# Order of the o statistics, the gate and the split remainders in a gated linear attention and FFN kernel

## What is computed

```python
def step(state, inp):                      # over the 512 positions, per head
    state = state * exp(gt)[..., None] + vt[..., None] * kt[..., None, :]
    return state, einsum('bhvk,bhk->bhv', state, qt)
out = (out - mean) / sqrt(var + 1e-05) * gamma + beta     # over 128 channels
out = (out * silu(x @ Wg)) @ Wout
x = layernorm(x + out)
h = silu(x @ w1.T * s1) * (x @ w2.T * s2)
h = gelu(h @ h1.T * t1)
h = gelu(h @ h2.T * t2)
x = layernorm(x + h @ w3.T * s3)
```

## Time and profile before

| | |
|---|---|
| median of 3 runs | 178.25 us (177.07 to 178.44) |
| the profiled execution | 178.06 us, of it the span 176.3 us |
| granted TensorE clock, mean | 0.998 of full |
| TensorE busy | 160.1 us (91%), 778 matmuls |
| TensorE weight loads | 119.9 us (68%) |
| VectorE busy | 137.3 us (78%) |
| ScalarE busy | 116.8 us (66%) |
| GpSimd busy | 111.8 us (63%) |

### The profile page before, as it was taken

The page is one execution under the profiler, slowest core; times in us unless marked ns, Lnnn a source line. Parts: engine busy times, 40 slices in busy tenths (PEclk is TensorE's granted clock), DMA queues, the critical chain, the costliest instruction groups (busy, mean ns, idle before and its releaser), DMA issues.

```text
span 176.3 us, 2661 instructions
## 1 busy us (share of the span) xinstructions
PE 160.1 (91%) x778; PEld 119.9 (68%) x778; DVE 137.3 (78%) x278; ACT 116.8 (66%) x211; POOL 111.8 (63%) x109
## 2 busy tenths in 40 slices
PE   0899999999888999998999999899999999999980
PEld 0766667868656676876868678587666875887870
DVE  0689889967798997599999975999996695854062
ACT  5444789993236836187787468677978578995721
POOL 8707987969907779983477998919684250803132
PEclk9999999999999999999999999999999999999999
DMA  4999910244100000000000000000002000040102
GB/s 111 329 396 414 393 48 0 51 129 121 60 4 0 2 0 0 4 0 2 0 0 0 0 0 0 0 0 0 0 0 65 0 0 0 2 114 23 55 8 63
DMA packets 7455, 10.55 MB, mean 60 GB/s; under 512 B 753, under 2 KB 5394, under 8 KB 6930
## 3 DMA queue, kind: packets, MB, share of 16 engines
q1 hardware_dynamic: 6866, 7.50, 13.8%
q0 software_dynamic: 576, 2.88, 4.2%
HBM read 8.55 MB, written 1.84 MB: 59 GB/s over the span
## 4 chain that ended last, share of the span: by engine, by line
POOL 18%; PE 14%; DVE 13%; issue 12%; ACT 6%; DVEq 1%; POOLq 0%; ACTq 0%
POOL u_tok L345 7%; DVE state L1152 5%; POOL f_lo L406 4%; PE ffn L667 3%; POOL o_acc L360 3%; PE ffn L658 2%; DVE y L1164 2%; PE ffn L636 2%; PE ffn L641 1%; ACT last_f L1108 1%; PE att L580 1%; POOL o_rstd L368 1%; POOL r_rstd L368 1%; PE ffn L682 1%; ACT f_hi L938 1%
## 5 line engine op out<-in xcount | busy, mean ns | idle before, releaser
L1152 DVE TENSOR_TENSOR_SCAN state<-gate,att 128x512 f32<-128x512 f32 x32 | 38.4, 1209 | 0.8 <-PE att L580 0.8
L406 POOL TENSOR_TENSOR f_lo<-full,f_hi 128x512 fp32r<-128x512 f32 x18 | 23.0, 1293 | 20.2 <-DVE full L1238 14.9
L946 ACT ACTIVATE f_hi<-ffn,vec_cols 128x512 fp32r<-128x512 f32 x24 | 16.5, 686 | 19.8 <-PE ffn L667 19.6
L658 PE MATMUL ffn<-f_hi,h_hi 128*128 128x512 f32 x96 | 28.2, 407 | 0.2
L667 PE MATMUL ffn<-f_lo,h_hi 128*128 128x512 f32 x96 | 26.1, 398 | 0.0
L360 POOL TENSOR_TENSOR o_acc<-o_acc,y 128x512 f32<-128x512 f32 x16 | 20.6, 1290 | 8.6 <-DVE y L1164 8.5
L345 POOL TENSOR_TENSOR u_tok<-kv_tok 128x1024 f32<-128x1024 f32 x12 | 25.5, 2136 | 0.1
L580 PE MATMUL att<-ident,u_tok 128*128 128x128 f32 x128 | 20.2, 285 | 2.1 <-POOL u_tok L345 1.3
L658 PEld LDWEIGHTS ffn<-f_hi,h_hi 128*128 128x128 f32 x96 | 17.6, 188 | 5.8 <-ACT f_hi L946 1.5
L580 PEld LDWEIGHTS att<-ident,u_tok 128*128 128x128 f32 x128 | 15.7, 146 | 7.3 <-DVE state L1152 2.9
L667 PEld LDWEIGHTS ffn<-f_lo,h_hi 128*128 128x128 f32 x96 | 17.8, 188 | 3.7
(11 more groups left out here) (188 smaller groups left out, 354.5 us busy)
## 6 DMA issues: line engine op xcount, KB each, us to landing
h_raw<-in_hT SPq DMA_DIRECT2D x2, 1024.0 KB, 12.0
h_hi<-in_hT POOLq DMA_DIRECT2D x2, 1024.0 KB, 11.6
x_tok<-in_x SPq DMA_DIRECT2D x4, 256.0 KB, 4.7
out<-out_tok SPq DMA_DIRECT2D x3, 256.0 KB, 2.3
w_raw<-in_w12T SPq DMA_DIRECT2D x1, 512.0 KB, 4.3
w_hi<-in_w12T POOLq DMA_DIRECT2D x1, 512.0 KB, 8.6
q_swap<-q_hi SPq DMA_DIRECT2D x3, 128.0 KB, 2.5
q_swap<-q_lo SPq DMA_DIRECT2D x3, 128.0 KB, 2.4
```

Source lines behind the costliest of these rows:

```text
L406: nc.gpsimd.tensor_tensor(lo[:, o], full_block(layer, o), hi[:, o].bitcast(F32), ALU.subtract).then_inc(pool_rested, 1)
L658: nc.tensor.matmul(bank[:], h_hi[:, layer - 1, c, tile(o)], src_hi[:, c], start=(c == 0), stop=False)
L946: nc.scalar.activation(hidden[layer][0][:, o], bank[:], ACT.Gelu, scale=scales[:, 1 + layer, o:o + 1]).then_inc(gelu_hi_ready, 1)
L1152: nc.vector.tensor_tensor_scan(state[:, k % 3], gate[:, b], A[2 + k % 2][:], 0.0, ALU.mult, ALU.add).then_inc(scanned, 1)
```

## The change

`transpose_o` is put ahead of `center_o`, and the statistics and the aggregate of o ahead of `apply_gate`. Two remainders change engines: (1,1) goes from GpSimd to VectorE, behind `apply_gate`; (2,3) from VectorE to GpSimd, behind the last outer product of the next row. rest(2,1) goes behind `x2_normalise`. On TensorE, x2's transposes go ahead of the output's pass over the rounded parts, and the next row's second set of u transposes and its first replicated q go ahead of `ffn_out_rest`. Two waits on ScalarE guard the slot `full[:, 0]`, which (2,3) now shares with (1,0) and with the next row's first silu.

```diff
--- before.py
+++ after.py
@@ -236,8 +236,8 @@
         weight_groups.append((flat(w3_raw[:]), flat(w3_hi[:]), flat(w3_lo[:]), (w3_loaded, w3_hi_loaded)))
         WG = len(weight_groups)
         ALL_BLOCKS = [(layer, o) for layer in range(3) for o in range(OB)]
-        ON_POOL = [(0, 0), (0, 1), (0, 2), (1, 0), (1, 1)]
-        ON_DVE = [(0, 3), (1, 2), (1, 3), (2, 1), (2, 0), (2, 2), (2, 3)]
+        ON_POOL = [(0, 0), (0, 1), (0, 2), (1, 0), (2, 3)]
+        ON_DVE = [(0, 3), (1, 2), (1, 1), (1, 3), (2, 0), (2, 1), (2, 2)]
         hidden = ((f1_hi, f1_lo), (f2_hi, f2_lo), (f1_hi, f1_lo))
         LAYER_2_BANK = (0, 2, 3, 1)
 
@@ -424,6 +424,8 @@
                 outer_products(a + 1, tiles)
                 r_rstd_of(a)
                 outer_products(a + 1, last_tiles)
+                if a >= 1:
+                    rest(a - 1, 2, 3)
                 if a >= 2:
                     e_var_of(a - 2)
                     e_rstd_of(a - 2)
@@ -431,7 +433,6 @@
             def ffn_middle(b, follows):
                 sum_over_k(b + 1, range(3, DH - 2))
                 rest(b, 1, 0)
-                rest(b, 1, 1)
                 if b >= 1:
                     e_minus_of(b - 1)
                 if follows:
@@ -757,9 +758,6 @@
                 last.then_inc(lo_count_ready, 1)
 
             def first_layer(b, f, with_lo, follows):
-                if follows:
-                    transpose_u(b + 1, 1)
-                    replicate_q(b + 1, 0)
                 ffn_in(b, 0, with_lo)
                 ffn_in(b, 1, with_lo)
                 if f is not None:
@@ -792,8 +790,8 @@
                 ffn_hidden(f, 1, 3, with_lo)
                 ffn_hidden_rest(f, 1, 3)
                 ffn_hidden(f, 2, 0, with_lo)
+                transpose_o(a)
                 center_o(a)
-                transpose_o(a)
                 ffn_hidden(f, 2, 1, with_lo)
                 project_out(a)
                 ffn_hidden_rest(f, 2, 0)
@@ -802,16 +800,20 @@
                 ffn_hidden_rest(f, 2, 2)
                 ffn_hidden(f, 2, 3, with_lo)
                 ffn_hidden_rest(f, 2, 3)
+                transpose_x2(a)
                 ffn_out_hi(f, with_lo)
-                transpose_x2(a)
                 if follows:
                     transpose_u(a + 1, 0)
+                    transpose_u(a + 1, 1)
+                    replicate_q(a + 1, 0)
                 ffn_out_rest(f)
                 first_layer(a, f, with_lo, follows)
 
             def rows(with_lo):
                 transpose_x2(0)
                 transpose_u(1, 0)
+                transpose_u(1, 1)
+                replicate_q(1, 0)
                 first_layer(0, None, with_lo, True)
                 with pe.Fori(0, B - 2) as i:
                     step(i + 1, i, with_lo, True)
@@ -926,6 +928,8 @@
 
             def ffn_silu(b, o):
                 act.wait_ge(a_ready, OB * b + o + 1)
+                if o == 0 and b >= 1:
+                    act.wait_ge(*rested(b - 1, 2, 3))
                 if o >= SLOTS:
                     act.wait_ge(f1_ready, OB * b + o - SLOTS + 1)
                     if (0, o - SLOTS) in ON_POOL:
@@ -946,6 +950,8 @@
                 nc.scalar.activation(hidden[layer][0][:, o], bank[:], ACT.Gelu,
                                      scale=scales[:, 1 + layer, o:o + 1]).then_inc(gelu_hi_ready, 1)
                 act.wait_ge(gelu_hi_ready, n)
+                if (layer, o) == (2, 3):
+                    act.wait_ge(*rested(b, 1, 0))
                 nc.scalar.activation(full_block(layer, o), bank[:], ACT.Gelu,
                                      scale=scales[:, 1 + layer, o:o + 1]).then_inc(gelu_ready, 1)
 
@@ -1303,18 +1309,18 @@
                 read_out(a, 7)
                 last_sums(a)
                 rest(f, 1, 2)
+                o_token_stats(a)
+                o_aggregate(a)
                 apply_gate(a)
-                o_token_stats(a)
+                rest(f, 1, 1)
                 rest(f, 1, 3)
-                o_aggregate(a)
 
             def make_x2(a, f):
                 add_x(a)
-                rest(f, 2, 1)
                 rest(f, 2, 0)
                 x2_normalise(a)
+                rest(f, 2, 1)
                 rest(f, 2, 2)
-                rest(f, 2, 3)
                 rest_of_x2(a)
             dve.sem_inc(out_ready, 1)
             dve.sem_inc(e_sum_ready, 1)
```

## The result

The changed kernel takes 178.50 us (median of 20 runs, 177.06 to 179.04), the kernel before 177.83 (20 runs, 177.07 to 178.61). The ratio is 1.0036, 95% interval [1.0019, 1.0054]: 0.64 us slower by the ratio and 0.67 by the medians, a little over a third of one per cent. 179.1 was forecast.

The account below looks back on a forecast made before the run. TensorE and VectorE were both near full, with the chain to o's rstd through GpSimd. Rows 1, 2 and 3 add 0.35 + 0.39 + 0.30 = 1.04 us to 178.06, giving 179.1; range 176.8 to 180.4.

Parts of the forecast that it names:

- GpSimd's part and o's statistics: Finishing o: one remainder less on GpSimd and transposes first bring o_rstd 1.25 us earlier, of which add_x keeps 0.99.
- the slower rival: Aggregate of o has a 0.28 us gap in each row, nothing absorbs it: 179.9, up to 180.5 us; chance 0.15.
- The gate's stall: At project_out, TensorE's weight loads wait 0.77 us for apply_gate behind the aggregate; everything queued up to (2,3)'s gelu shifts by 0.77.
- x2's rounding and the scans: On ScalarE, late gelus of (2,3) use up all slack: x2's rounding and the scans start 0.16 us later.
- the earlier transposes of u gain nothing: Before the scans: moving u's transposes earlier brings nothing, since scans start behind x2's remainder in both orders.
- The output's remainder behind replicate_q: At row's end, ffn_out_rest waits behind replicate_q(0): product 1 starts 3.75 us after rest_of_x2 instead of 3.56, +0.19.
- Product 0: Behind yT and its silu: needs 2.82 us after rest_of_x2 and has 2.84, so level.
- Row 1: First loop step: 0.35 us longer, with scans 0.16 later and product 1 another 0.19.
- Row 2: Second loop step, taken to repeat row 1: +0.35 us, plus 0.04 for a register instruction ahead of the gate.
- Row 3: Last loop step, no scans: GpSimd's rest(2,3) ends at 147.24, delaying ffn_out_rest's last load and making yT 0.30 us late.
- The clock: Rival: TensorE's clock falls to 1.2 GHz in the new stalls, +11 us in a row, over 185; chance 0.02.
- The wait at replicate_q(0) covers the others: On TensorE: its wait for rest_of_x2 hides ffn_out_hi's wait for rest(2,1), so that wait costs nothing.

Follow-up runs that it names:

- e1_q_back: Changed kernel with the next row's second u transposes and first replicated q moved back behind ffn_out_rest; ratio 0.9991 to the kernel before.
- e9_after_r21: Changed kernel with only rest(2,1) moved ahead of x2_normalise; ratio 1.0026 to the kernel before, loop 79.53 against 79.57 us in the changed kernel.
- e7_both_u1: Changed kernel with apply_gate between o's statistics and aggregate, and replicate_q(0) behind ffn_out_rest, second u transposes staying ahead; ratio 0.9970 to the kernel before.
- e8_r21: e7_both_u1 with rest(2,1) moved ahead of x2_normalise; ratio 0.9925 to the kernel before, the fastest measured.
- e2_gate_mid: Changed kernel with apply_gate moved between o's statistics and its aggregate; ratio 0.9988 to the kernel before.
- e3_both: Changed kernel with apply_gate between o's statistics and aggregate, and second u transposes and replicate_q(0) behind ffn_out_rest; ratio 0.9987 to the kernel before.

## Why the prediction was right, and where its steps were off

- **GpSimd's part and o's statistics:** right. o_mv, o_rstd and add_x came as reckoned: add_x 1.01 earlier (0.99 said), x2_normalise 1.00 (0.99). The aggregate ran with no gap inside (71.02, 0.38), so the slower rival's 0.28 did not come.
- **The gate's stall:** TensorE's loads waited 0.79 (0.77 said). But the gelu of (2,3) became late by 0.61, not 0.77: it starts 10.88 after o, before 10.27. I took the wait of the weight loads for that of the matmuls. project_out's loads ran ahead of its matmuls before, 71.78 and 72.01; after the stall both start at 72.09, and the matmuls' own idle is 0.36. After o the loads start 0.76 later than before, the matmuls 0.53, and the eight matmuls then take 1.16 instead of 1.05.
- **x2's rounding and the scans:** +0.16 said, 0.00 measured for the rounding and -0.07 for rest_of_x2. Besides the 0.61, the place before was misread. rest_of_x2 started at 81.34, 0.10 behind the rounding, because VectorE's own two remainders ended only then; there was a little more slack than I counted. The first scan starts 0.15 earlier after o (13.42 against 13.57), since it no longer starts behind the remainder's end (82.03 against 82.02) but 0.08 before it: "the earlier transposes of u gain nothing" was wrong by about this much, though no run has them alone. The timeline of before shows the two remainders:

```profile
80.14 1.28 DVE L1249 TENSOR_TENSOR f_lo<-ffn,f_hi 128x512 fp32r<-128x512 f32 x2
81.34 0.68 DVE L1232 TENSOR_TENSOR x_lo<-att,x_hi 128x512 fp32r<-128x512 f32 x1
```

- **The output's remainder behind replicate_q:** the mechanism was right and confirmed by e1_q_back; the term was 0.35 instead of 0.19. From the end of rest_of_x2 (80.82 + 0.69 = 81.51) to product 1 (85.42) it is 3.91, where 3.75 was said and 3.56 was reckoned for before (product 1 itself starts 3.54 behind it in that trace). Of the 0.16, 0.09 is replicate_q's load, 0.14 behind the remainder's end (81.65) instead of 0.05, and 0.07 product 1 behind its silu. Product 0, "level" by the prediction, came 2.98 behind the remainder (84.49), not 2.82.
- **Row 1:** +0.30 (0.35 said). That it came so close is luck: the scans' term was 0.16 too high or more, the output's 0.16 too low.
- **Row 2:** +0.02 (0.39 said). Of all steps this one failed most clearly: I copied row 1's terms. In row 2 o_rstd stood later (5.45 after o, 5.17 in row 1), behind GpSimd's e_minus as well, and ScalarE had 0.85 of idle ahead of the rounding, not 0.54. The timeline of before, row 2:

```profile
113.29 0.58 ACT L925 CAST x_hi<-att 128x512 fp32r<-128x512 f32 x1 [0.85 <-PE att L610]
```

The change takes x2's remainder from 13.19 to 12.84 after o there, 0.35 earlier, which the late yT then costs again: 115.78 - 100.64 = 15.14 after o against 14.55.

- **Row 3:** +0.19 (0.30 said). GpSimd's remainder is indeed what ends last ahead of ffn_out_rest, but follows the gelu that was late by 0.63 only. The last load of ffn_out_rest comes 0.72 later after o (147.04 - 133.31 against 146.45 - 133.44), yT only 0.19, because before, yT was not held by that load: ScalarE was at a table load until 146.22 + 1.28 = 147.50. The timelines of before and of after:

```profile
146.22 1.28 ACT L1027 ACT_TABLE_LOAD   x1
```

```profile
145.71 1.28 POOL L406 TENSOR_TENSOR f_lo<-full,f_hi 128x512 fp32r<-128x512 f32 x1 [3.14 <-ACT full L955]
...
147.04 0.19 PEld L683 LDWEIGHTS ffn<-f_lo,w_hi 128*128 128x128 f32 x1 [0.93 <-POOL f_lo L406]
```

- **The sum:** +0.67 by the medians and +0.51 in the loop, +1.04 said. Direction and mechanism held; the size was too large, and of the 0.53 between forecast and loop 0.37 are row 2's. Of the 0.6 between 179.1 and 178.50, 0.2 is the base: 178.06 was taken, the median of 20 runs is 177.83.
- **The clock:** the stages of after, with the columns of the earlier trace rows, show 1.00 through rows 1 and 2, the 2.4 GHz level, with the new stalls in them (row 3, 133.3 to 147.6, has 1.00 too). That rival is out for stalls of this size:

```profile
68.00:100.60 32.60, 31.36 (x151) 23.42 (x151) 29.20 (x56) 21.36 (x37) 23.57 (x20) 1.00 0.00 1
100.60:133.30 32.70, 31.45 (x152) 23.44 (x151) 29.26 (x56) 24.80 (x49) 25.11 (x22) 1.00 0.03 8
```

- **"The wait at replicate_q(0) covers the others":** right for the changed kernel (e9_after_r21), wrong as soon as the gate's stall is gone (e7_both_u1 against e8_r21). I took it over into the expectations of e2_gate_mid and e3_both without looking at it again. That was the larger part of their miss, 0.4 a row in e7_both_u1; the gate's remaining stall fits the rest.

What stays open: e3_both and e7_both_u1 differ by 0.5 us in the medians and by 0.01 in the loop; their intervals overlap. And no run parts GpSimd's remainder (2,3) from rest(1,1) on VectorE, so it isn't shown what each is worth in the fastest kernel. Nor was the gate put first again there.

## What to carry to other kernels

When a result is brought forward, follow what it was brought past: here the gate went behind o's aggregate, and TensorE's whole queue behind project_out paid for a reciprocal that came 1.25 us earlier. Price each pass of a loop from its own rows; the same place had 0.54 of slack in one pass and 0.85 in the next. And where several moves each look bad alone, take them back singly and together from the whole: the fastest version keeps most of the change and takes back three placements (the gate in part, replicate_q(0), rest(2,1)), of which the last gave 0.4 us a row once the other two were right, and nothing in the changed kernel.

## What the runs showed of the hardware

A wait in front of weight loads isn't what the work behind it loses. In the changed kernel the loads stood for 0.79 and the matmuls for 0.36. Before, the loads had run 0.23 ahead of the matmuls; after the stall both start at once, and the eight matmuls take 1.16 instead of 1.05. What followed was late by 0.61. In e7_both_u1 the loads stood for 0.34, the matmuls for nothing, the eight again took 1.16, and what followed was late by 0.17.
